# Two layer norms of a graph transformer, applied by ScalarE instead of VectorE

## What is computed

```python
for i in range(DEPTH):                                  # DEPTH = 4
    h = _layernorm(x, ln1_g[i], ln1_b[i])
    x = x + _linear_attn(h, Wq[i], Wk[i], Wv[i], Wo[i], bo[i])
    h = _layernorm(x, ln2_g[i], ln2_b[i])
    x = x + (gelu(h @ W1[i] + b1[i]) @ W2[i] + b2[i])
```

## Time and profile before

| | |
|---|---|
| runs before | 3489.51, 3498.57, 3504.27 us |
| span of the profiled execution, first to last instruction | 3482.0 us |
| what lies around the span in the three runs | 7.5 to 22.3 us |
| TensorE busy | 3221.5 us, 93% |
| VectorE busy | 2347.5 us, 67% |
| ScalarE busy | 1184.5 us, 34% |
| mean granted TensorE clock | 0.967 of full speed |

### The profile page before, as it was taken

The page is one execution under the profiler, slowest core; times in us unless marked ns, Lnnn a source line. Parts: engine busy times, 40 slices in busy tenths (PEclk is TensorE's granted clock), DMA queues, the critical chain, the costliest instruction groups (busy, mean ns, idle before and its releaser), DMA issues.

```text
span 3482.0 us, 43961 instructions
## 1 busy us (share of the span) xinstructions
PE 3221.5 (93%) x13869; PEld 2325.5 (67%) x13869; DVE 2347.5 (67%) x6155; ACT 1184.5 (34%) x2126; POOL 2056.9 (59%) x1776
## 2 busy tenths in 40 slices
PE   8888999999899999999889899898999998999989
PEld 6665667777677777767566666576666666665668
DVE  7998888854454555545677777676666666769951
ACT  3443333333233333323333334243342424422320
POOL 3330577777777777777377677773777777711100
PEclk9999999999999999999999999899999999999999
DMA  3422122222322222322355454454455555422125
GB/s 115 144 96 78 37 50 44 49 49 43 81 47 47 49 50 44 76 55 58 101 136 141 130 138 136 125 141 138 134 152 143 147 147 146 132 82 71 69 101 174
DMA packets 226182, 339.26 MB, mean 97 GB/s; under 512 B 51501, under 2 KB 179755, under 8 KB 225702
## 3 DMA queue, kind: packets, MB, share of 16 engines
q0 software_dynamic: 67840, 119.33, 16.2%
q1 hardware_dynamic: 119502, 162.08, 14.4%
q10 hardware_dynamic: 38616, 55.04, 5.0%
HBM read 248.16 MB, written 87.29 MB: 96 GB/s over the span
## 4 chain that ended last, share of the span: by engine, by line
PE 63%; DVE 21%; issue 5%; another core or an unknown queue 5%; POOL 2%; ACT 2%; DMA 1%; DVEq 1%; ACTq 0%; SPq 0%
PE bank_v L1817 16%; PE bank_a L1804 16%; PE bank_e L1859 8%; PE bank_v L1749 4%; PE bank_a L1721 3%; PE bank_v L1792 3%; PE bank_a L1643 3%; PE bank_v L1709 3%; PE bank_v L1967 2%; POOL arena L804 2%; DVE acc L1503 1%; DVE st L1080 1%; DVEq L1511 1%; DVE arena L1243 1%
## 5 line engine op out<-in xcount | busy, mean ns | idle before, releaser
L804 POOL DMA_INDIRECT arena<-gather_table,arena x880 | 954.7, 1085 | 456.2 <-issue 247.4
L846 POOL DMA_INDIRECT edge_records<-acc x800 | 969.3, 1212 | 402.9 <-issue 402.9
L1817 PE MATMUL bank_v<-W_sb,gT 128*125 128x256 f32 x3200 | 747.1, 385 | 18.3 <-issue 13.7
L1804 PE MATMUL bank_a<-hT,W_sb 128*128 128x500 f32 (+1 forms) x1664 | 716.1, 578 | 13.8 <-issue 12.3
L1817 PEld LDWEIGHTS bank_v<-W_sb,gT 128*125 128x125 f32 x3200 | 602.7, 191 | 122.0 <-issue 26.1
L1804 PEld LDWEIGHTS bank_a<-hT,W_sb 128*128 128x128 f32 x1664 | 317.4, 194 | 326.2 <-issue 307.2
L1859 PE MATMUL bank_e<-arena 128*125 128x260 f32 x1760 | 467.9, 410 | 5.6 <-issue 3.1
L881 ACT ACTIVATE gT<-bank_a,cols 128x500 f32<-128x500 f32 (+1 forms) x416 | 274.2, 661 | 466.1 <-PE bank_a L1804 375.1
L1859 PEld LDWEIGHTS bank_e<-arena 128*125 128x125 f32 x1760 | 327.5, 197 | 57.8 <-issue 7.7
L881 ACT ACTIVATE hT<-bank_a,cols 128x500 f32<-128x500 f32 (+1 forms) x208 | 145.6, 747 | 491.5 <-PE bank_a L1643 378.2
L1239 DVE TENSOR_TENSOR arena<-arena 128x1024 f32<-128x1024 f32 x220 | 268.3, 1220 | 0.0
(11 more groups left out here) (292 smaller groups left out, 4366.1 us busy)
## 6 DMA issues: line engine op xcount, KB each, us to landing
residual<-xs SPq DMA_DIRECT2D x60, 500.0 KB
xs<-residual SPq DMA_DIRECT2D x58, 500.0 KB
arena<-edge_rows ACTq DMA_DIRECT2D x220, 125.0 KB
queries<-qT_out SPq DMA_DIRECT2D x48, 500.0 KB
qT_in<-queries ACTq DMA_DIRECT2D x39, 500.0 KB
arena<-gather_table,arena POOLq DMA_INDIRECT x880
edge_records<-acc POOLq DMA_INDIRECT x800
slice_weights<-arena SPq DMA_DIRECT2D x12, 1000.0 KB, 5.0
```

Of the source, the lines that this page charges most:

```text
L804: e.indirect_dma_start(g_of(j)[:, i, :], None, table_d, bass.IndirectOffsetOnAxis(ap=node[:, TE * j + i:TE * j + i + 1].bitcast(I32), axis ...
L846: e.indirect_dma_start(rec_d, bass.IndirectOffsetOnAxis(ap=pos_i[:, f:f + 1], axis=0), r3[:, f, :], None).then_inc(d_rec, 16)
L1804: o = e.matmul(b[:, 0:n], W[:, k, f * P:(f + 1) * P], hv[:, k, 0:n], start=k == 0, stop=k == KC - 1)
L1817: o = e.matmul(b[0:R, i % 2 * D:(i % 2 + 1) * D], gv[:, f, i * R:(i + 1) * R], W2_sb[:, f * D:(f + 1) * D], start=f == 0, stop=f == FB - 1)
```

## The change

The two norms of the layers are applied by ScalarE. VectorE still makes the statistics, and then one more small instruction (`shift`), which writes -mean * rstd beside rstd. ScalarE writes rstd * x + shift with one Identity activation per tile, at the place in the list where VectorE's `apply` stood. The first norm's statistics move to a buffer of their own, `st_h`; the second norm's stay in `st`. The `join` norms stay on VectorE.

New waits: ScalarE waits for `ln2_scaled` or `h1_scaled` before it applies. VectorE waits for the previous apply of the same kind (`h2_set`, `h1_set`) before it takes new moments into the same statistics buffer, and for the apply of the same group before it adds b2 to the residual.

```diff
+            def apply(X, to, nt, stats):
+                for i in range(nt):
+                    o = e.activation(to[:, i, :], X[:, i, :], ACT.Identity, scale=stats[0:R, 56 + i:57 + i],
+                                     bias=stats[0:R, 60 + i:61 + i])
+                return o
...
+                elif stage == "ln2_apply":
+                    l, s = at
+                    e.wait_ge(ln2_scaled, nth(l, s))
+                    apply(by_tile(x_of(l + 1, s)[:, :]), by_tile(h2b[:, :]), tiles(s), st).then_inc(h2_set, 1)
+                elif stage == "h1_apply":
+                    l, s = at
+                    e.wait_ge(h1_scaled, NGR * l + s + 1)
+                    if s >= 2:
+                        e.wait_ge(v_done, v_end("context", l + 1, s - 2, KC - 1))
+                    else:
+                        e.wait_ge(v_done, v_end("context", l, NGR - 2 + s, KC - 1))
+                    apply(by_tile(x_of(l + 1, s)[:, :]), by_tile(h1_of(l + 1, s)[:, :]), tiles(s), st_h)\
+                        .then_inc(h1_set, 1)
...
+            def shift(nt, stats):
+                mv = stats[0:R, 32:32 + 2 * nt].rearrange("p (t k) -> p k t", k=2)
+                return e.scalar_tensor_tensor(stats[0:R, 60:60 + nt], mv[:, 0, :], -1.0, stats[0:R, 56:56 + nt],
+                                              ALU.mult, ALU.mult)
...
                     e.wait_ge(v_done, attend_end(l, s))
+                    if nth(l, s) > 1:
+                        e.wait_ge(h2_set, nth(l, s) - 1)
                     moments(by_tile(x_of(l + 1, s)[:, :]), tiles(s), st)
-                elif stage in ("ln2_scale", "h1_scale"):
+                elif stage == "ln2_scale":
                     step(scale(tiles(at[1]), st))
-                elif stage == "ln2_apply":
-                    l, s = at
-                    apply(by_tile(x_of(l + 1, s)[:, :]), by_tile(h2b[:, :]), tiles(s)).then_inc(h2_set, 1)
+                    shift(tiles(at[1]), st).then_inc(ln2_scaled, 1)
+                elif stage == "h1_scale":
+                    step(scale(tiles(at[1]), st_h))
+                    shift(tiles(at[1]), st_h).then_inc(h1_scaled, 1)
                 elif stage == "add_b2":
+                    e.wait_ge(h2_set, nth(l, s))
...
-                    moments(by_tile(x_of(l + 1, s)[:, :]), tiles(s), st)
-                elif stage == "h1_apply":
-                    l, s = at
-                    apply(by_tile(x_of(l + 1, s)[:, :]), by_tile(h1_of(l + 1, s)[:, :]), tiles(s)).then_inc(h1_set, 1)
+                    e.wait_ge(h1_set, nth(l + 1, s) - 1)
+                    moments(by_tile(x_of(l + 1, s)[:, :]), tiles(s), st_h)
```

More of the change, by code:

```diff
@@ L361, in build_program @@
         st = sb("st", [P, 64])
+        st_h = sb("st_h", [P, 64])
         st_x = [sb(f"st_x{i}", [P, 64]) for i in range(2)]
@@ L539, in build_program @@
         lg_set, pbd_set, x1_set = sem("lg_set"), sem("pbd_set"), sem("x1_set")
+        ln2_scaled, h1_scaled = sem("ln2_scaled"), sem("h1_scaled")
         q_exp, k_alpha, w_relu, w_exp, sw_exp, lg_exp = (sem("q_exp"), sem("k_alpha"), sem("w_relu"), sem("w_exp"),
@@ L1106, in apply @@
                 for i in range(nt):
-                    o = e.tensor_scalar(to[:, i, :], X[:, i, :], st[0:R, 32 + 2 * i:33 + 2 * i],
-                                        st[0:R, 56 + i:57 + i], ALU.subtract, ALU.mult)
-                return o
+                    o = e.tensor_scalar(to[:, i, :], X[:, i, :], st_h[0:R, 32 + 2 * i:33 + 2 * i],
+                                        st_h[0:R, 56 + i:57 + i], ALU.subtract, ALU.mult)
+                return o
+            def shift(nt, stats):
+                mv = stats[0:R, 32:32 + 2 * nt].rearrange("p (t k) -> p k t", k=2)
+                return e.scalar_tensor_tensor(stats[0:R, 60:60 + nt], mv[:, 0, :], -1.0, stats[0:R, 56:56 + nt],
+                                              ALU.mult, ALU.mult)
             def input_statistics(s):
@@ L1541, in _ @@
                     e.wait_ge(join_set, s + 1)
-                    moments(x1, nt, st)
-                    step(scale(nt, st))
+                    if s == 0:
+                        e.wait_ge(h1_set, nth(LAST, END))
+                    moments(x1, nt, st_h)
+                    step(scale(nt, st_h))
                     apply(x1, by_tile(h3_of(s)), nt).then_inc(h1_set, 1)
```

## The result

The changed kernel takes 3522.15 us, the median of four runs (3520.56 to 3525.85), beside 3498.58 us for the kernel before on the same chip: the ratio is 1.0070, with an interval of 1.0051 to 1.0089. That is 24 us slower. The prediction said 3523.

The account below looks back on a forecast made before the run. TensorE's own work, busy 93% of the span, was taken as the bound. Terms 11.1 + 4.9 + 2.5 + 3.4 + 4.0 + 7.5 - 6.1 = 27, less 2, gave +25 us: 3498.57 to 3523 us, range 3496 to 3548.

Parts of the forecast that it names:

- Apply: One Identity activation on ScalarE: 0.50 us, 2.0 us for four tiles, 175 us in all.
- END: First norm beside 250-column `up` blocks, once in each of three layers: TensorE stands for a late bank, 11.1 us.
- Sort: First norm at two places where sort instructions on VectorE delay the statistics: TensorE stalls, 4.9 us together.
- Group 1's second norm: At layer starts, applies and a table load ahead of the layer's first eviction make TensorE wait: 2.5 us.
- Four edge places: First norm among edge blocks, with Relu, Exp and table loads behind the apply: 0.2 to 1.4 us each, 3.4 together.
- Transposes that wait for the apply: Group 0's second norm in four layers, first norm of END in three: TensorE waits longer, 4.0 us.
- Relief: VectorE's freed time shortens TensorE's waits at queries and edge blocks: 6.1 us gained, bounds 0 and 59.6.
- Clock: TensorE's clock falls after the five new stalls at END and Sort: 1.5 us each, 7.5 us.
- The usual place: Some 25 of 39 first norms: the eviction of `up` 2 fits with 0.8 us to spare, 0 us.
- (a): Rival, no difference: clock falls after few stalls, applies cost 0.42 us, idle time only moves; about 3505 us, chance 0.30.
- (b): Rival, faster: VectorE's free time reaches the edge blocks, up to 31 us there; about 3480 us, chance 0.10.
- (c): Rival, much slower: The usual place stalls too, 20 to 25 us more; about 3546 us, chance 0.13.

Follow-up runs that it names:

- h1_twice: The changed kernel with each apply of the first norm made twice in a row on ScalarE: 3459.12 us, ratio 1.0221 to the kernel before.
- later: The changed kernel with ScalarE's applies later: first norm's ahead of `up` 4, group 1's second norm's ahead of `up` 2; 3369.31 us, ratio 0.9962 to before.
- h1_on_act: The kernel before with only the first norm applied by ScalarE, the second staying on VectorE: 3511.65 us, ratio 1.0044.
- no_apply: The kernel before with both applies of the layers left out, a tiny VectorE copy giving the signal: 3479.19 us, ratio 0.9966.
- after_third: The changed kernel once more, unaltered, on the chip of the third set: 3534.17 us, ratio 1.0067 to the kernel before.
- third set: Repeat runs on another chip, beside 29 runs of the kernel before at 3511.55 us.
- later_again: The kernel of later run again in the third set: 3513.15 us, ratio 1.0005 to the kernel before.
- before_third: The kernel before, unchanged, run and profiled in the third set: 3510.06 us, ratio 0.9997.
- first set: Runs on one chip, beside 27 runs of the kernel before at 3493.84 us.

## Why the prediction came out right, and which terms did not

The chain of reasoning held: ScalarE's evictions wait behind an apply that waits for the statistics, and TensorE stands where the bank three places back is late. h1_twice shows the mechanism, later removes it, h1_on_act places most of it. Term by term, from the first trace of the changed kernel unless said otherwise:

- **Apply, 0.50 us**: 0.52 (2.07 for four), so 182 us of ScalarE in place of 175. An estimate from the Trainium skill, page "ScalarE: Activation LUTs", section "What ACT_TABLE_LOAD costs", is 186 + 2 x 93 + 0.833 x 256 = 585 ns for one by itself; the trace agrees, with a mean of 592 ns.
- **END, 11.1**: 3.26 + 3.36 + 4.82 = 11.4. **Sort, 4.9**: 2.30 + 2.52 = 4.8. Right to 0.3 us; the other two traces have 11.4 and 12.6, 4.9 and 4.7.
- **Group 1's second norm, 2.5**: 3.05 + 2.56 + 2.59 = 8.2, so mis-sized (7.0 and 6.9 in the other two traces). I had moved VectorE and ScalarE and not TensorE. At the start of the second layer, counted from the first transpose of `h2`, the first eviction ended at 10.9 us, as reckoned (10.8), but TensorE wanted the bank at 8.4 and not at 10.0. It came to the `up` blocks after 2.8 us instead of 3.7, since the wait for the queries' norm behind the transposes (`gT L1379`, 4.6 us in four layers) had vanished, while VectorE's moments of group 1 still begin at 2.8, when the transposes of `h2` have been taken out. Net of the 4.6 the places cost 3.6.
- **Four edge places, 3.4**: nothing in sum. All waits of `up` together grew by 37.0 - 12.5 = 24.5 us, and the eight places make 24.4; the short ones, nearly all among edge blocks and up to 2.09 us, come to 12.6 us where they came to 12.5. Between traces of the unchanged kernel they differ by 6 us, so a term of 3.4 is not excluded, but not seen either.
- **Transposes that wait for the apply, 4.0**: 20.6 + 3.1 - 19.1 = 4.6. (3.1 us of rows 10's 19.1 are the `join` norm, which the change leaves alone.)
- **Relief, -6.1**: no_apply puts the part that the change can have at about 6 us, but with bounds of 0 and 12. The queries' 4.6 us are no part of it: with nothing applied these waits came to 6.1 us. They vanished in the changed kernel, where TensorE waits longer for ScalarE's apply and VectorE meanwhile goes on to the queries.
- **Clock, 7.5**: the term that varies. TensorE's busy time in the first two layers was 1.2 us longer than before in the first trace (from the rows by stage, 570.48 + 566.45 to 573.52 + 564.59) and 9.0 longer in after_third; the three traces of the unchanged kernel lie within 3.5 us of each other. The 1.5 us a stall was about right (1.7 in a row) where the clock fell; that it falls after every stall was wrong.
- **The usual place, 0**: no stall, with 0.5 to 1.0 us to spare where I had reckoned 0.8.

The terms, with the measured sizes and the clock of one or the other trace, make 11.4 + 4.8 + 8.2 + 4.6 - 4.6 + (1 to 9) = 25 to 33 us, less the relief of about 6 us (0 to 12): 19 to 27. The measured loss is 24 us, and 23.5 by the ratio of the third set. The 2 us that I took off for other waits that shrink were not measured by themselves. So +25 was met partly by luck, because errors of 3 to 6 us had opposite signs: group 1 too small, the edge places and the clock too large.

**Rivals.** (a) had the mechanism for the clock partly right, but the stalls' idle time did not move elsewhere: three comparisons give 1.0070, 1.0042 and 1.0067, two of them wholly or nearly wholly above 0.5%, the second astride it. (b) falls with no_apply. (c) did not happen and was 0.5 to 1.0 us away at each of some 25 places. The rule of the Trainium skill named with it ("ScalarE: Activation LUTs", section "Rules for kernel authors": multiplications and additions belong on VectorE) pointed to the right side, but its reason, that VectorE is faster per number (its figure is for bf16, the numbers here are fp32), is not what cost here: with the same 350 activations at later places (later_again) the ratio is 1.0005.

**Open**: why **later** gains 0.4% on one chip and nothing on the other. Ahead of the edge stage it is 4.1 us shorter than before_third on the third set (1374.0 to 1369.9), its edge stage is 5.8 longer, and no second trace of before on that chip says how far the stage varies there; on the other chip no trace of before was taken. How much of the edge stage's growth in the first set was the change's stays open too. What decides whether the clock falls after a stall of 2.5 us wasn't tried.

## What to carry to other kernels

Handing work to an engine that is idle two thirds of the time cost nothing here by its length, and 24 us by its place: ask what that engine does next for the bound engine, when its operands will be ready, and how many buffers lie between. Here there are three banks, so an eviction may come late by two blocks of 1.68 us less its own 0.68, that is 2.7 us, for the wait for the statistics and the applies together; the same apply two `up` blocks later, with the statistics mostly there, cost nothing that could be measured. And before putting an engine's lateness down as a gain to be had, take its work out altogether once: 131 us off VectorE were worth 12, about 6 of them from the waits for the apply itself.

## What had not been expected of the hardware

- The chips differ more than the change does: the kernel before has medians of 3381, 3494, 3499 and 3512 us, on the fastest with a granted clock of 0.977 in the changed kernel's trace where it is 0.968 in the first one. There the edge stage of the changed kernel is 1289 us long (645.6 + 643.1), and 1407 and 1420 in its other two traces, while the layers without edges are alike (604.0 us for the first, 604.5 and 609.2 elsewhere). Only ratios to before on the same chip can be compared.
- The same stall of 2.5 us at the same instruction is followed by full clock in one execution and by 0.68 in another.
